# A perceiver layer on one core: keys transposed by DMA, value mixing packed on column tiles, new orders

## The chip, the cores and the metric

The kernel runs on one core of one Trainium2 chip. The time is the device time of one execution in microseconds (us), the median of several. A core has a matrix engine (TensorE, PE in the profile), a vector engine (VectorE, DVE), an activation engine (ScalarE, ACT), a general engine (GpSimd, POOL) and a queue engine (SyncE, SP), each with its own instruction stream, executed in order; they wait for one another by semaphores. SBUF is the on-chip memory, PSUM the memory that TensorE writes.

## The reference

x is 64 batches of 64 tokens of 128 numbers, the context 64 batches of 128 tokens of 96. Three blocks, each with a residual, follow one another:

```python
x = x + xattn(layernorm(x), ctx)   # 16 heads of 64, softmax over 128 context tokens, @ Wo + bo
x = x + attn(layernorm(x))         # 16 heads; scores from 5 sigmoid "path" bits a head: a tree similarity, causal softmax
x = x + ffn(layernorm(x))          # product-key experts: 8 heads; q@K1, q@K2 (32 keys each), the 10 best of the
                                   # 32x32 sums, softmax over them, gelu(x.w_down) weighted, times w_up
```

## The kernel before

The 4096 tokens are worked in 32 tiles of 128 tokens (two batches), t = 0 to 31. Every tile goes through some 100 named steps. `x.*` is the cross attention up to the probabilities (`x.q` queries, `x.w` their copies to SBUF, `x.s` scores, `x.x` maxima, `x.e` exponentials, `x.r` and `x.n` the division, `x.p` transposes of the probabilities, `x.t` their copies), `y.*` the mixing of the context and its output, `t.*` the tree attention, `k.*` the key scores and the choice of the best, `e.*` the experts: for each head h `e.s` adds the two key scores of all 1024 experts by a 0/1 matrix, `e.x` takes the exponential, `e.w` masks what is under the cut, `e.a` adds the heads up. The number in a name is a group of four heads (x, y) or a head (e).

The five order tables at the end of the file (`PE_ORDER` and so on, lines 1122 to 1148) set everything: `run` goes through iterations i, and in each one through the table's names in order; a name with lag L works on tile i - L. So one iteration, a period, holds steps of up to eight tiles, and each engine's instruction stream is fixed by its table. `BANK` (line 1151) gives each PE result its part of PSUM: x0, x1, t0, t1 (512 columns each), f0, f1 (1024 each). The waits at the head of a PE step, such as `after(pe, "y.u2", t - 1)`, wait until the previous user of that part has been read. Waits at the edges only (`at_ends`) don't matter inside.

The steps that the change touches:

- `keys_turn` (line 507), PE: eight transposes of 128x128 fp16 blocks of `us`, the key scores split into a high and a low fp16 part (`k.split`, line 949), into PSUM bank t1; `keys_sb` (line 642), ACT: one copy of the 128x1024 result to `usT`. The eight `e.s` of the tile use `usT` as weights (line 571).
- `mix` (line 384), PE: the transposed probabilities of a group times the context, one product of 96 rows of output and 512 columns (8 heads by 64 queries); `mix_sb` (line 630), ACT: the copy into `uT`, 96 partitions.
- `cross_out` (line 394), PE: a bias product and 16 products, one for each head, of 96 contracted rows. An fp32 product appears in the profile as two records.
- `queries`, `scores`, `probs_turn`, `sums`, `w_turn` and others: only which earlier step they wait for, with the new banks.
- SP's loads (lines 225 to 243): constants, then 16 small pieces of `awo`, then the steady loads `ld.x`, `ld.ct`, `ld.c`, `ld.xr` and the store `st.y`. ACT's queue loads six more weights (lines 652 to 657).
- the setup of the key weights and the fp16 split of the experts' `wdT` on DVE (`setup_keys`, line 828), done ahead of `y.res` of tile 0.

Of the kernel before, what the change touches and what calls it, by code (L numbers as in the profile page):

```python
# [8 lines left out]
M, CD = 128, 96  # L9
# [7 lines left out]
XHP, AHP = XH // 2, AH // 2  # L17
EC = NE // 128
# [10 lines left out]
def build(nc, a):  # L29
# [3 lines left out]
    with ctx:  # L33
# [3 lines left out]
        def sem(name):  # L37
# [24 lines left out]
        vo = sb("vo", [CD, XH, D])  # L62
# [20 lines left out]
        uT = sb("uT", [CD, XH, 2, N])  # L83
# [42 lines left out]
        own = {n: sem(n) for n in """wqk_load wvo_load key_load bias_load tree_load expert_load ones_set pool_set  # L126
            setup_ps setup_sb qk_split key_sb parts_done split_done
# [13 lines left out]
        def run(steps, order, begun=(), once={}):  # L141


            assert set(order) == set(steps), set(order) ^ set(steps)
            for i in range(NT + depth):
                for name, lag in order.items():
                    t = i - lag
                    if t == 0 and name in once:
                        once[name]()
                    if 0 <= t < NT and not (t == 0 and name in begun):  # L150
                        steps[name](t)
# [33 lines left out]
        def _(sp):  # L185
# [31 lines left out]

            def store(t):
# [11 lines left out]
            load_xr(0)  # L230
            sp.dma_start(bias[:, 512:640], a["bo"]).then_inc(own["bias_load"], 16)
            sp.dma_start(bias[:, 640:720], a["bp"]).then_inc(own["bias_load"], 16)
            for dst, name in ((wp, "wp"), (awv, "awv"), (rootc, "rootc"), (cneg, "cneg"), (ident16, "ident16")):
                sp.dma_start(dst[:], a[name]).then_inc(own["tree_load"], 16)
            sp.dma_start(wdT[:], a["wdT"]).then_inc(own["expert_load"], 16)
            sp.dma_start(sel[:], a["sel"]).then_inc(own["expert_load"], 16)
            sp.dma_start(wup[:], by_chunk(a["wup"])).then_inc(own["expert_load"], 16)
            for r in range(2):
                for c in range(AHP):
                    h = 2 * c + r  # L240
                    sp.dma_start(awo[N * r + AD * c:N * r + AD * c + AD, :], a["awo"][AD * h:AD * h + AD, :])\
                        .then_inc(own["tree_load"], 16)
            run(steps, SP_ORDER, begun=("ld.x", "ld.ct", "ld.c", "ld.xr"))
# [3 lines left out]
        def _(pe):  # L247
# [9 lines left out]
            def setup_vo():  # L257
                pe.wait_ge(own["wvo_load"], 16 * 2)
                pe.wait_ge(own["qk_split"], 4)
                for j in range(4):  # L260
                    if j >= 2:
                        pe.wait_ge(own["setup_sb"], j + 3)
                    head_pairs(j, wvT, wo, D, CD).then_inc(own["setup_ps"], 1)
# [93 lines left out]
            def probs_turn(k):  # L357
                def step(t):
                    if k == 0:
                        pe.wait_ge(s["x.e3"], t + 1)  # L360
                    elif k == 1:
                        pe.wait_ge(s["y.u0"], t + 1)
                    elif k == 2:
                        pe.wait_ge(s["x.e1"], t + 1)
                    elif k == 3:
                        after(pe, "t.csb", t - 1)
                        at_ends(pe, "x.w3", t)
# [6 lines left out]
            def mix(k):  # L374
                def step(t):
# [6 lines left out]
                    elif k == 3:  # L382
# [3 lines left out]
                    done(f"y.m{k}", pe.matmul(bank[BANK[f"y.m{k}"]][0:CD, :], c0[:, t % 2, k // 2, :], pT[:, k, :],  # L386
                                              start=True, stop=True))
# [6 lines left out]
            def cross_out(t):  # L394
                pe.wait_ge(s["y.u3"], t + 1)
                if t == 0:
                    pe.wait_ge(own["setup_sb"], 8)
                    pe.wait_ge(own["split_done"], 1)
# [10 lines left out]
            def t_turn(t):  # L409
                after(pe, "k.ksb", t - 1)  # L410
                at_ends(pe, "y.res", t)
                pe.wait_ge(s["t.norm"], t + 1)
                done("t.turn", pe.transpose(bank[BANK["t.turn"]][:, 0:128], xn2[:, t % 2, :], ident[:]))
            steps["t.turn"] = t_turn

            def paths_values(t):
# [16 lines left out]
            def feat_turn(t):  # L433
                pe.wait_ge(s["t.path"], t + 1)
                after(pe, "x.w3", t + 1)
                at_ends(pe, "t.sb", t)
# [45 lines left out]
            def tree_out(t):  # L482
                pe.wait_ge(s["t.div"], t + 1)
# [10 lines left out]
            def key_scores(t):  # L494
                pe.wait_ge(s["k.high"], t + 1)
                pe.wait_ge(s["k.low"], t + 1)
                if t == 0:
                    pe.wait_ge(own["key_sb"], 2)
                    pe.wait_ge(own["split_done"], 2)
# [7 lines left out]
            def keys_turn(t):  # L507
                after(pe, "y.res", t + 1)
                at_ends(pe, "t.csb", t)
                if t == 0:  # L510
                    pe.wait_ge(own["tree_load"], 16 * 21)
                pe.wait_ge(s["k.split"], t + 1)
                out = bank[BANK["k.kturn"]].bitcast(f16)
# [690 lines left out]
```

## Time and profile before

| | |
|---|---|
| runs | 1131.19, 1133.36, 1134.92 us; median 1133.36 |
| profiled execution | 1133.51 us, of it the span from the first to the last instruction 1131.7 us |
| granted TensorE clock, mean | 0.973 of full speed |
| busy | PE 89%, DVE 78%, ACT 85%, POOL 73% of the span |
| start, 31 periods, end | 69, 1009, 53 us |

A period is the time from a step of one tile to the same step of the next. Busy time is the union of an engine's instructions; idle time of an engine is shown with the instruction that ended it. The ends of matrix products are modelled, so consecutive groups on PE overlap in their shown times; the distance from start to start is what a group occupies.

### The profile page before, as it was taken

To read this page: it belongs to the slowest core of one execution; us is meant where nothing else is said; L and a number is where in the kernel's file an instruction comes from. 1 tells how busy PE (TensorE), PEld (TensorE's weight loads), DVE (VectorE), ACT (ScalarE), POOL (GpSimd) and SP (SyncE) were. 2 spreads that over 40 slices of the span, in tenths; PEclk is the share of its full clock that TensorE was granted. 3 is DMA by queue.
4 is the path that set the end of the run, shared out by engine and by line. 5 is a ranking of instruction groups with operands and counts; after the bars stand their busy time and mean duration, and the time that the engine had idled before them with its cause. 6 is when DMAs were issued, how large, how long until landed. Compare 5 with 4: busy or idle time off the path is not lost.

```text
span 1131.7 us, 34471 instructions
## 1 busy us (share of the span) xinstructions
PE 1009.9 (89%) x11656; PEld 771.8 (68%) x11656; DVE 883.9 (78%) x2941; ACT 960.1 (85%) x2251; POOL 824.9 (73%) x871
## 2 busy tenths in 40 slices
PE   3789899999999999999999999999999999999755
PEld 3666677777766777776677777766776777667433
DVE  2447788888888888888888888888888888888763
ACT  2579899999999999999999999999998999998642
POOL 0137777777987777788777777887777779777755
PEclk9999999999999999999999999999999999999865
DMA  6000000000000000000000000000000000000000
GB/s 158 13 13 12 14 15 4 16 16 16 17 13 16 11 9 16 16 16 14 16 16 7 13 16 17 16 14 16 17 4 16 16 16 15 13 14 7 4 3 6
DMA packets 36684, 18.79 MB, mean 17 GB/s; under 512 B 13632, under 2 KB 36256, under 8 KB 36512
## 3 DMA queue, kind: packets, MB, share of 16 engines
q1 hardware_dynamic: 32832, 14.91, 4.8%
q10 hardware_dynamic: 3680, 1.67, 0.6%
q8 instruction: 97, 1.59, 0.6%
q14 instruction: 75, 0.61, 0.2%
HBM read 14.47 MB, written 2.10 MB: 15 GB/s over the span
## 4 chain that ended last, share of the span: by engine, by line
DVE 29%; PE 27%; POOL 17%; issue 14%; ACT 10%; SPq 1%; DVEq 1%; POOLq 0%; DMA 0%; ACTq 0%
POOL wsum L1111 10%; PE psXT L386 9%; ACT p L698 6%; DVE mw L1003 6%; POOL feat L1095 5%; DVE cand L974 5%; DVE top L942 4%; DVE best L969 3%; DVE best L979 3%; PE psXT L351 3%; PE psXT L441 3%; PE psF L571 2%; PE psXT L370 2%; ACT am L737 2%; DVE us L954 1%
## 5 line engine op out<-in xcount | busy, mean ns | idle before, releaser
L1111 POOL TENSOR_TENSOR wsum<-wsum,mw 128x1024 f32<-128x1024 f32 x192 | 451.7, 2353 | 165.0 <-DVE mw L1003 159.4
L1003 DVE SCALAR_TENSOR_TENSOR mw<-psF,cut,ew 128x1024 f32<-128x1024 f32 x256 | 325.8, 1281 | 56.8 <-ACT ew L788 53.0
L788 ACT ACTIVATE ew<-psF,lnz 128x1024 f32<-128x1024 f32 x256 | 288.3, 1127 | 13.3 <-PE psF L571 10.2
L698 ACT ACTIVATE p<-psXT,negmax 128x128 f32<-128x128 f32 x512 | 182.2, 387 | 2.5 <-DVE negmax L876 2.5
L571 PE MATMUL psF<-sel,usT 128*128 128x512 f16 x512 | 157.0, 389 | 23.4 <-DVE mw L1003 20.4
L351 PE MATMUL psXT<-cT,q 96*128 96x128 f32 x1024 | 140.4, 281 | 22.8 <-ACT p L698 18.2
L351 PEld LDWEIGHTS psXT<-cT,q 96*128 96x128 f32 x1024 | 128.4, 194 | 42.9 <-ACT p L698 33.8
L1062 POOL TENSOR_TENSOR p<-p,rrow 128x512 f32<-128x512 f32 x128 | 131.2, 1035 | 19.0 <-DVE rrow L885 19.0
L386 PE MATMUL psXT<-pT,c 128*96 128x512 f32 x256 | 134.2, 611 | 0.8 <-ACT pT L604 0.8
L404 PE MATMUL psXT<-vo,uT 96*128 96x128 f32 x1024 | 121.2, 277 | 0.0
L698 ACT ACTIVATION_READ_ACCUMULATOR p<-psXT,negmax 128x1 f32 x512 | 117.2, 229 | 0.0
L404 PEld LDWEIGHTS psXT<-vo,uT 96*128 96x128 f32 x1024 | 116.9, 192 | 0.0
L286 PE MATMUL psXT<-xnT,qk 128*96 128x128 f16 x512 | 93.3, 223 | 8.3 <-DVE xnT L867 8.2
L1049 POOL TENSOR_TENSOR rstd<-mv,halfneg 128x1 f32<-128x1 f32 x96 | 52.7, 549 | 60.7 <-DVE mv L853 60.2
L876 DVE TENSOR_REDUCE negmax<-psXT 128x4 f32<-128x512 f32 x128 | 85.7, 669 | 12.0 <-PE psXT L351 11.8
L287 PE MATMUL psXT<-xnT,qk 128*96 128x128 f16 x512 | 93.1, 222 | 0.0
L288 PE MATMUL psXT<-xnT,qk 128*96 128x128 f16 x512 | 93.0, 222 | 0.0
L942 DVE MAX8 top<-psXT 128x8 f32<-128x32 f32 x512 | 53.3, 181 | 42.9 <-PE psXT L288 42.9
L370 PEld LDWEIGHTS psXT<-ident,p 128*128 128x128 f32 x512 | 62.9, 142 | 31.8 <-ACT uT L604 14.9
L604 ACT ACTIVATE uT<-psXT 96x512 f32<-96x512 f32 x128 | 75.3, 590 | 5.5 <-PE psXT L386 2.3
L1111 POOL TENSOR_TENSOR wsum<-mw 128x1024 f32<-128x1024 f32 x32 | 75.6, 2362 | 3.9 <-DVE mw L1003 3.9
L370 PE MATMUL psXT<-ident,p 128*128 128x128 f32 x512 | 77.5, 274 | 0.5 <-ACT p L698 0.5
(132 smaller groups left out, 2265.1 us busy)
## 6 DMA issues: line engine op xcount, KB each, us to landing
cT<-cT_dram SPq DMA_DIRECT2D x32, 96.0 KB, 2.0
c<-c_dram SPq DMA_DIRECT2D x32, 96.0 KB, 2.0
x<-x_dram SPq DMA_DIRECT2D x32, 64.0 KB, 2.2
xr<-x_dram SPq DMA_DIRECT2D x32, 64.0 KB, 1.8
y_dram<-y SPq DMA_DIRECT2D x32, 64.0 KB, 2.4
wqT<-wqT_dram SPq DMA_DIRECT2D x1, 512.0 KB, 5.9
wo<-wo_dram ACTq DMA_DIRECT2D x1, 512.0 KB, 9.8
wdT<-wdT_dram SPq DMA_DIRECT2D x1, 512.0 KB, 6.6
```

What stands on the lines that cost most here:

```text
L286: pe.matmul(out, left[:, 0, :], right[:, 0, :], start=not open_group, stop=False)
L351: mm = pe.matmul(bank[BANK[f"x.s{k}"]][:, i * M:i * M + M], q[:, b, h:h + 2, :].rearrange("c h q -> c (h q)"), cT[:, t % 2, b, :], start=T ...
L370: mm = pe.transpose(bank[BANK[f"x.p{k}"]][:, i * 128:i * 128 + 128], p[:, k, i, :], ident[:])
L386: done(f"y.m{k}", pe.matmul(bank[BANK[f"y.m{k}"]][0:CD, :], c0[:, t % 2, k // 2, :], pT[:, k, :], start=True, stop=True))
L404: mm = pe.matmul(out, uT[:, h, :, :].rearrange("c b q -> c (b q)"), vo[:, h, :], start=False, stop=(h == XH - 1))
L571: mm = pe.matmul(bank[BANK[f"e.s{h}"]][:, j * 512:j * 512 + 512], usT[:, t % 4, h, :], sel[:, j * 512:j * 512 + 512], start=True, stop=True)
L698: ins = act.activation(p[:, k, i, :], bank[BANK[f"x.s{k}"]][:, i * M:i * M + M], ACT.Exp, bias=negmax[:, k, i:i + 1], accum_out=rowsum[:, ...
L788: done(f"e.x{h}", act.activation(ew[:, h % NEW, :], bank[BANK[f"e.s{h}"]], ACT.Exp, bias=lnz[:, t % 4, h:h + 1]))
L942: ltop.link(dve.max(top[:, t % 2, k, :], keyed[:, k, :]))
L1003: done(f"e.w{h}", dve.scalar_tensor_tensor(out=mw[:, h % NMW, :], in0=bank[BANK[f"e.s{h}"]], scalar=cut[:, t % 4, h:h + 1], in1=ew[:, h % ...
L1062: done(f"x.n{k}", pool.tensor_tensor(p[:, k, :, :], p[:, k, :, :], rrow[:, k, :].unsqueeze(2).to_broadcast([128, 4, M]), ALU.mult))
L1111: done(f"e.a{h}", pool.tensor_tensor(wsum[:, t % 2, :], mw[:, 0, :] if h == 1 else wsum[:, t % 2, :], mw[:, h % NMW, :], ALU.add))
```

## The change

The keys' transpose becomes a step of SP, one transposing DMA a tile, from `us` to `usT`; PE's and ACT's steps for it are gone. The packed mixing: the contraction of 96 rows a head in `cross_out` is laid out over all 128 partitions. Of each four heads, three keep partitions 0 to 95 of their own slot, and the fourth's 96 rows are cut in three pieces of 32, one on partitions 96 to 127 of each slot; so `uT` and `vo` have 12 slots of 128 partitions. `mix` writes this layout by six products on column tiles. `y.u` copies 128 partitions by 384 columns. The orders, lags and banks of all engines are new, and with them the waits. In the start, loads are issued in the order of their use, `x` of tile 1 sixth, `awo` in two pieces, `wvT`, `wo`, `fwqT`, `fbqT` and `keys` from SP's queue; the DVE setup moves to `t.div` and `k.top` of tile 0.

```diff
-        vo = sb("vo", [CD, XH, D])
+        vo = sb("vo", [128, XH3, D])                 # XH3 = 12
-        uT = sb("uT", [CD, XH, 2, N])
+        uT = sb("uT", [128, XH3, 2, N])
+            def keys_turn(t):                        # on SP
+                sp.wait_ge(s["k.split"], t + 1)
+                for h in range(FH):
+                    after(sp, f"e.s{h}", t - 4)
+                after(sp, "k.kturn", t - 1)
+                sp.nop(nofuse=True)
+                sp.dma_start(usT[:, t % 4], us[:].rearrange("p h a b -> p (h a b)"), transpose=True)\
+                    .then_inc(s["k.kturn"], 16)
             load_x(0)
             sp.dma_start(wqT[:], by_chunk(a["wqT"])).then_inc(own["wqk_load"], 16)
             sp.dma_start(ident[:], a["ident"]).then_inc(own["wqk_load"], 16)
             load_ct(0)
             load_c(0)
-            load_xr(0)
+            load_x(1)
+            sp.dma_start(wvT[:], by_chunk(a["wvT"])).then_inc(own["wvo_load"], 16)
+            sp.dma_start(wo[:], by_chunk(a["wo"])).then_inc(own["wvo_load"], 16)
...
             def mix(k):                              # y.m
...
-                    done(f"y.m{k}", pe.matmul(bank[BANK[f"y.m{k}"]][0:CD, :], c0[:, t % 2, k // 2, :], pT[:, k, :],
-                                              start=True, stop=True))
+                    probs = pT[:, k, :].rearrange("m (g j q) -> m g j q", g=2, j=4)
+                    to = bank[BANK[f"y.m{k}"]][:, 0:6 * N].rearrange("c (g j q) -> c g j q", g=2, j=3)
+                    for j in range(3):
+                        cols = c0[:, t % 2, k // 2, 32 * j:32 * j + 32]
+                        pe.matmul(to[32 * j:32 * j + 32], cols, probs[:, :, 0:3, :], start=True, stop=True,
+                                  tile_position=(0, 32 * j))
+                        mm = pe.matmul(to[96:128, :, j, :], cols, probs[:, :, 3, :], start=True, stop=True,
+                                       tile_position=(0, 96))
+                    done(f"y.m{k}", mm)
...
             def cross_out(t):
-                for h in range(XH):
-                    mm = pe.matmul(out, uT[:, h, :, :].rearrange("c b q -> c (b q)"), vo[:, h, :],
-                                   start=False, stop=(h == XH - 1))
+                for i in range(XH3):
+                    mm = pe.matmul(out, uT[:, i, :, :].rearrange("c b q -> c (b q)"), vo[:, i, :],
+                                   start=False, stop=(i == XH3 - 1))
...
-            def keys_turn(t):                        # on PE
-                after(pe, "y.res", t + 1)
-                for h in range(FH):
-                    mm = pe.transpose(out[:, h * 128:h * 128 + 128], us[:, h, :, :].rearrange("p a b -> p (a b)"),
-                                      ident16[:])
...
             def mix_sb(k):                           # y.u
-                    to_sb(eng, f"y.u{k}", uT[:, 8 * (k % 2):8 * (k % 2) + 8, k // 2, :],
-                          bank[BANK[f"y.m{k}"]][0:CD, :].rearrange("c (h q) -> c h q", h=8))
+                    to_sb(eng, f"y.u{k}", uT[:, 6 * (k % 2):6 * (k % 2) + 6, k // 2, :],
+                          bank[BANK[f"y.m{k}"]][:, 0:6 * N].rearrange("c (i q) -> c i q", i=6))
...
-            def keys_sb(t):                          # on ACT
-                to_sb(eng, "k.ksb", usT[:, t % 4].rearrange("p h t -> p (h t)"), bank[BANK["k.kturn"]].bitcast(f16))
...
 PE_ORDER = {
+    "e.s2": 5, "e.s1": 5, "x.q3": 3, "x.s1": 3, "e.s0": 5, "t.fturn": 4, "e.s3": 5, "x.s3": 3, "t.sim": 4,
+    "e.s4": 5, "e.wturn": 6, "t.mix": 4, "x.p0": 3, "e.s5": 5, "t.cturn": 4, "x.p2": 3, "t.out": 4, "x.p1": 3,
+    "e.s6": 5, "y.m0": 3, "y.m2": 3, "y.m1": 3, "k.turn": 4, "e.s7": 5, "x.p3": 3, "k.key": 4, "y.m3": 3,
+    "x.turn": 2, "e.hid": 4, "y.out": 3, "x.q0": 2, "x.q1": 2, "e.out": 6, "x.q2": 2, "t.turn": 3, "x.s2": 2,
+    "t.pv": 3, "x.s0": 2,
 ACT_ORDER = {
+    "t.pexp": 4, "x.e2": 3, "k.lnz": 5, "e.x2": 5, "e.x1": 5, "x.e0": 3, "e.x0": 5, "t.fsb": 4, "e.x3": 5,
+    "x.e1": 3, "t.exp": 4, "e.x4": 5, "x.e3": 3, "x.t0": 3, "t.csb": 4, "e.x5": 5, "x.t2": 3, "x.t1": 3, "e.x6":
+    5, "k.norm": 4, "y.u2": 3, "k.high": 4, "y.u0": 3, "y.u1": 3, "x.t3": 3, "x.norm": 2, "e.x7": 5, "y.u3": 3,
+    "x.high": 2, "e.gelu": 4, "k.shift": 4, "x.w0": 2, "x.w1": 2, "t.norm": 3, "x.w2": 2, "t.sb": 3, "k.eb": 4,
+    "t.v": 3,
 DVE_ORDER = {
+    "e.add": 7, "k.z": 5, "t.path": 4, "x.x0": 3, "x.w3": 3, "e.w2": 5, "x.r2": 3, "e.w1": 5, "x.x1": 3, "x.r0":
+    3, "e.w0": 5, "e.w3": 5, "x.x3": 3, "x.r1": 3, "e.gate": 6, "t.div": 4, "e.w4": 5, "x.r3": 3, "t.res": 4,
+    "e.w5": 5, "x.stats": 1, "k.low": 4, "e.w6": 5, "k.top": 4, "k.split": 4, "x.low": 2, "e.w7": 5, "y.res": 3,
+    "k.cand": 4, "x.x2": 2,
 POOL_ORDER = {
+    "e.a7": 6, "t.feat": 4, "x.n2": 3, "x.n0": 3, "e.a1": 5, "x.n1": 3, "e.a2": 5, "x.n3": 3, "k.root": 4,
+    "e.a3": 5, "e.a4": 5, "e.a5": 5, "k.inner": 4, "e.a6": 5, "t.root": 3, "x.root": 1,
 SP_ORDER = {
-    "ld.x": 0, "st.y": 7, "ld.ct": 2, "ld.c": 2, "ld.xr": 2,
+    "st.y": 7, "ld.ct": 2, "ld.c": 2, "k.kturn": 4, "ld.x": 0, "ld.xr": 2,
```

The orders of before stand in the tables of the kernel (PE, for comparison: e.s1, x.s3, e.s0, t.fturn, x.s1, e.s3, t.sim, e.wturn, e.s4, x.p0, t.mix, e.s5, x.p2, t.cturn, y.m0, t.out, x.p3, y.m2, x.p1, e.s7, y.m3, k.turn, y.m1, x.turn, k.key, e.hid, y.out, e.s6, x.q1, x.q0, k.kturn, x.q2, e.out, x.s2, t.turn, t.pv, e.s2, x.s0, x.q3).

## Rows read from the trace of the kernel before

**Rows 1.** The instructions of line 485 (`t.out`): durations, first and last start

```profile
L485 PE MATMUL psXT<-awo,actxT x64: 275/287/422, 69.2 to 1078.5; 128*128 128x128 f32 x64
```

**Rows 2.** Windows view: one period; busy PE, PEld, DVE, ACT, POOL; granted clock; DMA share

```profile
600.24:632.79 32.55, 30.44 (x364) 23.42 (x363) 27.21 (x92) 29.71 (x71) 25.75 (x28) 1.00 0.06 15
```

**Rows 3.** Timeline of PE: start us, us shown, line, result<-operands, count

```profile
602.91 0.61 PE L515 MATMUL psXT<-ident,us 128*128 128x128 f16 x8
...
603.36 0.22 PE L286 MATMUL psXT<-xnT,qk 128*96 128x128 f16 x1
...
624.77 0.60 PE L370 MATMUL psXT<-ident,p 128*128 128x128 f32 x4
...
625.21 0.59 PE L571 MATMUL psF<-sel,usT 128*128 128x512 f16 x2
...
626.78 1.04 PE L386 MATMUL psXT<-pT,c 128*96 128x512 f32 x2
...
627.66 0.27 PE L300 MATMUL psXT<-ident,xn 128*128 128x128 f32 x1
...
630.07 3.79 PE L404 MATMUL psXT<-vo,uT 96*128 96x128 f32 x32
...
633.69 0.60 PE L571 MATMUL psF<-sel,usT 128*128 128x512 f16 x2
```

**Rows 4.** Chain of waits in that period: start us, us, what

```profile
602.56 1.19 DVE best L969 x8
...
607.16 1.29 DVE mw L1003
...
628.97 1.67 DVE top L942 x16
```

**Rows 5.** Timeline of ACT in the same period

```profile
603.56 1.02 ACT L604 ACTIVATE usT<-psXT 128x1024 f16<-128x1024 f16 x1 [0.53 <-PE psXT L515]
...
610.15 0.36 ACT L698 ACTIVATE p<-psXT,negmax 128x128 f32<-128x128 f32 x1
...
611.52 1.14 ACT L788 ACTIVATE ew<-psF,lnz 128x1024 f32<-128x1024 f32 x1
...
623.56 0.58 ACT L604 ACTIVATE uT<-psXT 96x512 f32<-96x512 f32 x1
...
630.27 1.28 ACT L778 ACT_TABLE_LOAD   x1 [0.65 <-PE psF L288]
...
633.90 0.60 ACT L759 ACTIVATE cand<-psXT 128x512 f32<-128x512 f32 x1
```

**Rows 6.** Timeline of PE around the tree's tiled steps

```profile
616.68 1.16 PE L454 MATMUL psXT<-featT 32*64 32x64 f32 x64
...
617.77 1.09 PE L583 MATMUL psF<-ident,wsum 128*128 128x128 f32 x8
...
619.13 0.60 PE L370 MATMUL psXT<-ident,p 128*128 128x128 f32 x4
...
619.69 1.11 PE L470 MATMUL psXT<-v,am 64*64 64x9 f32 x64
...
620.74 0.61 PE L571 MATMUL psF<-sel,usT 128*128 128x512 f16 x2
```

**Rows 7.** DMA issues: queue, size, median us from issue to landing

```profile
xr<-x_dram SPq DMA_DIRECT2D x32, 64.0 KB, 1.8
...
sel<-sel_dram SPq DMA_DIRECT2D x1, 256.0 KB, 6.9
```

**Rows 8.** Timelines of DVE and PE in the start

```profile
20.45 0.29 DVE L848 BATCH_NORM_STATS2 st<-x 128x6 f32<-128x128 f32 x1 [6.32 <-DMA x<-x_dram]
...
21.57 0.31 PE L286 MATMUL psXT<-xnT,qk 128*96 128x128 f16 x1 [8.24 <-DVE xnT L867]
...
44.52 3.79 PE L404 MATMUL psXT<-vo,uT 96*128 96x128 f32 x32
...
51.12 0.28 DVE L897 TENSOR_TENSOR x<-xr,psXT 128x128 f32<-128x128 f32 x1
```

More of the change, by code:

```diff
@@ L149, in run @@
                         once[name]()
-                    if 0 <= t < NT and not (t == 0 and name in begun):
+                    if 0 <= t < NT and (name, t) not in begun:
                         steps[name](t)
@@ L237, in _ @@
             sp.dma_start(wup[:], by_chunk(a["wup"])).then_inc(own["expert_load"], 16)
[L238 to L243, printed above, removed]
+            run(steps, SP_ORDER, begun=(("ld.x", 0), ("ld.x", 1), ("ld.ct", 0), ("ld.c", 0), ("ld.xr", 0)))
             sp.wait_ge(s["st.y"], 16 * NT)
@@ L482, in tree_out @@
             def tree_out(t):
-                pe.wait_ge(s["t.div"], t + 1)
+                pe.wait_ge(s["t.csb"], t + 1)
                 pe.wait_ge(s["t.csb"], t + 1)
@@ L551, in step @@
                     elif h == 2:
[L552 to L553 removed]
+                        pe.wait_ge(s["e.gelu"], t + 1)
                     elif h == 3:
@@ L578, in w_turn @@
             def w_turn(t):
-                after(pe, "e.w0", t + 1)
-                at_ends(pe, "e.w6", t)
+                after(pe, "e.w3", t + 1)
+                at_ends(pe, "e.add", t - 1)
                 pe.wait_ge(s[f"e.a{FH - 1}"], t + 1)
@@ L640, in copies @@
                         steps[name] = step
-            def keys_sb(t):
-                eng.wait_ge(s["k.kturn"], t + 1)
-                for h in range(FH):
-                    after(eng, f"e.s{h}", t - 4)
-                to_sb(eng, "k.ksb", usT[:, t % 4].rearrange("p h t -> p (h t)"), bank[BANK["k.kturn"]].bitcast(f16))
-            if "k.ksb" in order:
-                steps["k.ksb"] = keys_sb
         @block.scalar
@@ L1128 @@
+    "t.pv": 3, "x.s0": 2,
 }
 ACT_ORDER = {
-    "e.x1": 5, "x.e0": 3, "e.x0": 5, "t.fsb": 4, "e.x3": 5, "x.e3": 3, "t.exp": 4, "x.e1": 3, "x.t0": 3, "e.x4":
-    5, "t.csb": 4, "x.t2": 3, "y.u0": 3, "e.x5": 5, "x.t3": 3, "x.t1": 3, "k.norm": 4, "y.u2": 3, "k.high": 4,
-    "y.u3": 3, "y.u1": 3, "e.x7": 5, "x.high": 2, "e.gelu": 4, "k.shift": 4, "x.norm": 1, "x.w1": 2, "k.ksb": 4,
-    "x.w0": 2, "e.x6": 5, "t.norm": 3, "x.w2": 2, "t.sb": 3, "k.eb": 4, "t.v": 3, "k.lnz": 4, "t.pexp": 3,
-    "e.x2": 4, "x.e2": 2,
[3 rows of a table added]
@@ L1135 @@
+    "x.high": 2, "e.gelu": 4, "k.shift": 4, "x.w0": 2, "x.w1": 2, "t.norm": 3, "x.w2": 2, "t.sb": 3, "k.eb": 4,
+    "t.v": 3,
 }
 DVE_ORDER = {
-    "x.x0": 3, "x.w3": 3, "e.w2": 5, "e.w1": 5, "x.x3": 3, "x.r0": 3, "e.w0": 5, "x.x1": 3, "e.w3": 5, "x.r3":
-    3, "x.r2": 3, "e.gate": 6, "x.stats": 1, "x.r1": 3, "t.div": 4, "e.w4": 5, "t.res": 4, "e.w5": 5, "k.low":
-    4, "k.top": 4, "x.low": 2, "k.split": 4, "e.w7": 5, "y.res": 3, "k.cand": 4, "e.w6": 5, "k.z": 4, "e.add":
-    6, "x.x2": 2, "t.path": 3,
+    "e.add": 7, "k.z": 5, "t.path": 4, "x.x0": 3, "x.w3": 3, "e.w2": 5, "x.r2": 3, "e.w1": 5, "x.x1": 3, "x.r0":
@@ L1164 @@
 DVE_BIAS = "x.x2"
-DVE_KEYS = "y.res"
+DVE_KEYS = "t.div"
+DVE_DOWN = "k.top"
 def kernel(**inputs):
```

192 lines of the change are left out of this document (94 added, 98 removed), and 10 rows, old and new, of the table BANK.

## The prediction

> **What bounds the kernel now.** I read the repeated step first. Output matmul `t.out` starts first at 69.2 us, and its last record, the second of its product, at 1078.5 us [rows 1]: 31 periods of 32.55 us, 1009 of the 1131.7 us of the span. So the question is what one period becomes; before it lie 69 us, behind it 53 us. The windows view of one period shows no engine that is always busy: PE 30.4, ACT 29.7, DVE 27.2, POOL 25.8 of 32.55 us, TensorE's granted clock 1.00, that is 2.4 GHz, DMA 6% [rows 2]. PE's busy time is flattered by a tail: four transposes `x.p` show 0.60 us, but what follows starts 0.44 us after them [rows 3]; so 0.16 us of each group is pipeline. I use start to start throughout. So counted PE occupies about 29.4 us, ACT 29.7, and DVE, with the gaps inside its chains, some 27.7 to 28.5. The period is 3 us longer than any engine's work: it is a cycle that runs over several engines, each with a fixed order. The chain of waits shows it: `k.cand` (4.60 us from start to the next mask), the mask `e.w6`, later `k.top` [rows 4], with POOL's features and PE's mixes between. A change helps if it shortens that cycle or allows a shorter one.
>
> **The change in the period, part by part.**
> (1) PE's eight key transposes go: 8 in 0.45 us [rows 3]. ACT's copy goes: 1.02 us, some 0.92 start to start, and the 0.53 us that ACT idled ahead of it [rows 5].
> (2) `cross_out` has 12 head products in place of 16. 32 records take 3.62 us [rows 3], 0.113 each (two records a product), so 8 fewer save 0.90.
> (3) ACT's `y.u` reads 384 columns in place of 512. 1024 columns take 1.02 us and 512 take 0.58 [rows 5], 0.86 ns a column, so 0.11 us each, 0.44 in four.
> (4) The mix, most uncertain. Now one product of 512 columns, 0.88 us [rows 3]. Then six products on four column tiles, three of 384 and three of 128 columns: 1536 columns if one follows another, 384 on the fullest tile. At 0.88/512 us a column that is 2.64 us or 0.66. What tiles do side by side shows in the tree steps: 64 records of 64 columns on four tiles take 1.09 us, 17 ns each; 64 records of only 9 columns take 1.05, 16 ns each [rows 6]. A full-array record of 128 columns takes 113 ns, so one of 64 would take 57. Two row groups alone could bring that to 28, not to 17: column tiles do overlap, and both steps look bound by issue. Twelve records at 17 ns are 0.2 us of issue, no bound here. Proved is only 1.6 times what one stream does in one row group, so the bounds are 0.66 and 2.64/1.6 = 1.65 us. I take 0.66, nearest to what those rows do, and 0.1 us for each change into and out of tiles (x.p starts at 619.13, takes 0.44, and `t.mix` starts at 619.69 [rows 6]). `y.m0, y.m2, y.m1` stand together and `y.m3` apart, so four such gaps: 4 x 0.66 + 0.4 = 3.04 us against 3.52, a gain of 0.5; the bounds are 0.5 gained and 3.5 lost.
> The Trainium skill (TensorEngine Tiling (Array Packing), Key Properties) says that a change of tiling mode drains TensorE; the gap in rows 6 agrees. It also lists fast weight load as off under column tiling; if that made every weight load visible, the mixes would lose rather than gain, which is the first rival.
> (5) The transpose by DMA, 256 KB on SP's queue. No row shows a transposing DMA. Plain ones: 64 KB land in 1.8 us, 256 KB in 6.9 beside the other start loads [rows 7]. I take 5 us, bounds 1.8 and, if eight 128x128 blocks went one after another at 1.8 each, 14.4. Cover: `k.split` ends near 23.5 us in the walk below, `e.s2` is wanted at 31.3 and its consumer not before 33, so 7.8 to 9 us cost nothing. Meanwhile DVE does `e.w7`, `y.res` and `k.cand`. On SP the waiting issue stands ahead of `ld.x` and `ld.xr`, whose data are wanted most of a period later, and of the next store; none waits on the path.
> The Trainium skill speaks against this part: VectorE: DVE Perf Modes, The three transpose paths, gives 1309 ns for one 128x128 by DMA and 390 ns by TensorE; eight times the first is 10.5 us, an estimate beyond the cover, by which the period would grow by 1.5 to 2.7 us. Advanced Engine Details and Errata, X-Bar Transpose (TRN2), says that these DMAs are as fast as regular ones, which would leave it hidden. No row decides between them.
> (6) The orders. I walk the new cycle with start-to-start times. From the end of `x.x2` on DVE, ACT runs without a gap: four `x.e` at 1.37, five `e.x` at 1.00 (1.14 shown, 0.14 of it overlapped) [rows 5], `t.fsb` and `t.exp` 1.0 and 0.9 as steps of 1024 columns too, `x.t0` 0.48 (0.58 less 0.1 overlapped), two short `t.csb` 0.57, `k.lnz` 0.15: 13.6 us. PE then runs `t.out` 0.3, `x.p1` and `x.p3` 0.44 each, `e.s6` and `e.s7` 0.43 each, three mixes 2.64 at today's price, `k.key` (four products of 512 fp16 columns, 0.21 each) 0.86, `y.m3` 0.88, two small transposes 0.27, `e.hid` 24 x 0.056 = 1.35 [rows 3]: 8.0. ACT: two table loads, gelu and the step to `k.shift`'s start 3.63 [rows 5], `k.shift` 0.5. DVE: `k.cand` 4.60 [rows 4], `x.x2` 0.6. With four hand-overs of 0.1 to 0.2: 13.6 + 8.0 + 4.1 + 5.2 + 0.6 = 31.5 us. The old copy is in none of these legs; the path features, which now start the period on DVE and POOL, no longer wait behind `e.a6`. In the same walk `y.out` (2.8 us) ends just as `e.w7` does, POOL (25.8 us of work) is ready wherever it is asked, and `x.s1` costs a wait of about 1 us for the copy `x.w3` that sits directly ahead of it, which ACT's leg covers. With the mixes of (4) the cycle is 31.0; a hand walk misses waits, so I add 0.2: **31.2 us**, 1.35 less than now, 42 us over 31 periods.
>
> **The start.** The second x tile is asked for behind 32 other issues; DVE stands 6.32 us for it until 20.45, and the first query products start at 21.57 [rows 8]. With it sixth, `x.low` follows ACT's copy at 13.7, and the queries at about 14.2: 7.3 us. `wvT` and `wo` move to SP, land by some 14, and are wanted after the queries, four us later. The key and expert setup on DVE holds `y.res` of tile 0 until 51.12 though the cross output (44.52 + 3.79) is there at about 48.3 [rows 8]: 2.8 us; moved to `t.div` and `k.top` it meets a DVE that waits for PE, at a cost I put at 1. Sum 9, bounds 4 and 12. The tail keeps its POOL chain of seven sums; 0, bounds -3 and +3.
>
> **Sum.** The profiled execution took 1133.5 us (span 1131.7 and 1.8 around it), as the median of the runs, 1133.4. 1133.5 - 42 - 9 = 1082.5, say **1083 us**. Its own range is a period of 30.6 to 31.8, 1063 to 1103.
>
> **Rivals.**
> First, *column tiles overlap only in part*, the slower side. For it: all six products of a mix read the full 128 rows, the second record of a product waits for the first on its tile (0.33 us for 384 columns), and what queues behind it may not start; then a mix is 3 x (0.33 + 0.11) = 1.32 us. Against it: such a blocking would give the tree's 64-column records 28 ns, not 17 [rows 6]. All four mixes are in PE's leg, so the period is 31.7 (31.5 and the 0.2) + 4 x 0.44 + 0.4 = 33.9, the time 1133.5 + 31 x 1.3 - 9 = 1165 us; at 1.65 us a mix the period is 35.2 and the time 1206. It decides against the change from a period of 32.84, where the start's 9 us are used up: a mix of about 1.07 us beside the gaps.
> Second, *the DMA is late*. At 14.4 us it exceeds the 9 us by 5.4, the period is 36.6, the time 1250; slower from a landing of 10.6 us on. For it: nothing in the trace but the want of a row; against it: DMA engines at 6% [rows 2] and 64 KB in 1.8 us [rows 7]. By the skill's 10.5 us and a cover of 9 the same arithmetic gives 32.7 and 1129 us.
> Third, *the new order has waits of its own* that the walk doesn't see, `x.s1`, the three mixes waiting for `x.t2` and `x.t1`, whose copies follow `e.x5`. The period would be 32.2, the time 1133.5 - 11 - 9 = 1113. For it: three engines then have 28.0 to 28.5 us of work each, and evenly loaded engines leave less room to catch up; today's slack over the fullest engine, 2.9 us, would alone give 31.3.
> That the transposing DMA doesn't replace the PE and ACT steps isn't a case: both are gone from the program.
>
> **How the numbers follow.** Forecast 0.59, better still (period under 30.6) 0.06, third rival 0.18, first 0.11, second 0.06. A measurement of this kernel can tell 0.3%, 3.4 us. Of the third rival 0.03 falls within 3.4 us of before and 0.01 beyond: faster 0.79, same 0.03, slower 0.18. Range 1056 to 1128: it leaves out 0.02 below and 0.17 to 0.18 above, the two slower rivals.
>
> **What would show it.** The period, from the first and last `t.out`: near 31.2. Start to start of the mixes: 0.66 right, above 1.07 the first rival. The landing of the `usT` DMA: under 8 us, and no wait of `e.s2` for it; above 10, the second. ACT with no idle from `x.e2` to `t.csb`; DVE idle ahead of `k.cand` for `k.shift`. The first queries near 14 us. I am wrong if PE idles more than 3 us in a period for causes other than these.

## The result, and the profile after

| | before | after |
|---|---|---|
| median of four runs, us | 1133.2 (1131.2 to 1134.9) | 1119.9 (1118.7 to 1122.6) |
| ratio, 95% interval | | 0.989 (0.986 to 0.991) |
| profiled execution, us (span) | 1133.5 (1131.7) | 1122.6 (1119.4) |
| span's start to the first `t.out`, us | 69.2 | 60.6 |
| period, first to last `t.out`, over 31 | 32.56 | 32.53 |
| last `t.out` to the end, us | 53.2 | 50.3 |

The change gained 13 us, where 50 were forecast. In the profiled executions the start gave 8.6, the tail 2.9, the 31 periods together 1. First the records of `t.out` (line 519), to be held against [rows 1]:

```profile
L519 PE MATMUL psXT<-awo,actxT x64: 275/347/554, 60.6 to 1069.1; 128*128 128x128 f32 x64
```

In the windows view, with the columns of [rows 2], stand two neighbouring periods, and a stretch inside the second:

```profile
567.64:599.74 32.10, 29.06 (x386) 23.62 (x386) 27.39 (x92) 27.94 (x70) 25.89 (x27) 1.00 0.09 22
599.74:632.63 32.89, 30.35 (x386) 24.83 (x386) 27.41 (x93) 28.19 (x70) 25.91 (x27) 0.95 0.10 22
604.60:608.00 3.40, 3.40 (x17) 2.73 (x15) 2.60 (x4) 3.10 (x7) 2.16 (x3) 0.51 0.00 0
```

The work did leave: ACT has 27.9 us where [rows 2] show 29.7, PE 29.1 for 30.4. Yet the faster period is only 0.45 us shorter than before, and the slower one has a hole in TensorE's clock: 3.4 us at 0.51, that is 1.2 GHz. Between 100 and 1030 us the kernel before has one such stretch, this one has twelve, on 12 of 29 periods. From one `t.out` to the next the periods that a hole touches last 32.92 us in the mean, the others 32.13 (tiles 2 to 29). What stands around the hole, in PE's timeline (start, us, line, what; in brackets the idle time before it and its releaser), first in the undisturbed period:

```profile
567.98 0.60 PE L589 MATMUL psF<-sel,usT 128*128 128x512 f16 x2 [0.42 <-DVE y L1030]
...
570.43 1.13 PE L377 MATMUL psXT<-cT,q 96*128 96x128 f32 x8 [1.18 <-DMA cT<-cT_dram]
...
571.93 0.61 PE L589 MATMUL psF<-sel,usT 128*128 128x512 f16 x2 [0.37 <-DVE mw L1012]
572.38 1.04 PE L475 MATMUL psXT<-ident,feat 128*64 128x128 f32 x8
573.25 0.59 PE L589 MATMUL psF<-sel,usT 128*128 128x512 f16 x2
...
602.53 1.13 PE L377 MATMUL psXT<-cT,q 96*128 96x128 f32 x8 [1.18 <-DMA cT<-cT_dram]
...
604.03 0.61 PE L589 MATMUL psF<-sel,usT 128*128 128x512 f16 x2 [0.37 <-DVE mw L1012]
604.47 1.85 PE L475 MATMUL psXT<-ident,feat 128*64 128x128 f32 x8
606.12 1.06 PE L589 MATMUL psF<-sel,usT 128*128 128x512 f16 x2
```

In both periods PE waits three times in some five microseconds: 0.42 us ahead of `e.s1`, 1.18 ahead of `x.s1`, 0.37 ahead of `e.s0`. In one of them the clock then falls, and `t.fturn` takes 1.65 us start to start in place of 0.87. The long wait is the one of the third rival, for the copy `x.w3` on DVE; it ends at 602.39, just before `x.s1` starts. The profile writes "DMA cT" against it, the last of several semaphores, but no load of this tile's keys is under way there:

```profile
601.72 0.67 DVE L626 TENSOR_SCALAR q<-psXT 96x512 f32<-96x512 f32 x1
```

ACT in the undisturbed period, for [rows 5]:

```profile
589.84 1.28 ACT L785 ACT_TABLE_LOAD   x1 [0.88 <-PE psF L314]
...
593.47 0.60 ACT L766 ACTIVATE cand<-psXT 128x512 f32<-128x512 f32 x1
...
599.26 0.27 ACT L773 ACTIVATE ebest<-best 128x80 f32<-128x80 f32 x1 [2.09 <-DVE cut L993]
```

and DVE's `k.cand` in it, for the first row of [rows 4], with POOL's `e.a7` beside it:

```profile
594.20 1.18 DVE L978 MAX8 best<-cand 128x8 f32<-128x72 f32 x8 [0.48 <-ACT cand L766]
...
598.50 0.52 DVE L991 TENSOR_TENSOR cut<-best 128x8 f32<-128x8 f32 x1
599.06 0.17 DVE L993 TENSOR_SCALAR cut<-cut 128x8 f32<-128x8 f32 x1
599.14 0.69 DVE L885 TENSOR_REDUCE negmax<-psXT 128x4 f32<-128x512 f32 x1
599.74 0.28 DVE L1030 TENSOR_TENSOR y<-x,psF 128x128 f32<-128x128 f32 x1
```

```profile
596.64 2.35 POOL L1120 TENSOR_TENSOR wsum<-wsum,mw 128x1024 f32<-128x1024 f32 x1
```

`k.cand` lasts 4.94 us until `x.x2`, not 4.60. One instruction did it: the sum over 8 elements on line 991 took 0.52 us and ended within 0.03 us of POOL's addition. Before, POOL stood idle there: its next addition starts at 608.59, after 5.02 us without work, and `k.cand` ends at 607.16. All 32 of each kernel, with min/median/max in ns:

```profile
L982 DVE TENSOR_TENSOR cut<-best x32: 171/171/173, 86.3 to 1096.1; 128x8 f32<-128x8 f32 x32
```

```profile
L991 DVE TENSOR_TENSOR cut<-best x32: 171/528/685, 79.0 to 1085.7; 128x8 f32<-128x8 f32 x32
```

The transposing DMA, in the view of [rows 7], and the start, for [rows 8]:

```profile
usT<-us SPq DMA_TRANSPOSE x32, 3.2
```

```profile
12.26 0.28 DVE L857 BATCH_NORM_STATS2 st<-x 128x6 f32<-128x128 f32 x1
...
40.94 0.29 DVE L906 TENSOR_TENSOR x<-xr,psXT 128x128 f32<-128x128 f32 x1 [2.57 <-PE psXT L439]
```

```profile
13.38 0.31 PE L312 MATMUL psXT<-xnT,qk 128*96 128x128 f16 x1 [1.82 <-DVE xnT L876]
```

256 KB land, transposed, in 3.2 us (median of 32), and no step of PE waits for them. DVE no longer stands for the x tile, the first queries start 8.2 us earlier, and `y.res` of tile 0 waits for PE in place of the reverse.

### The profile page after: what moved, and what is told of

Read it like the earlier page. It is cut to its first block and busy times, and to the rows that moved or that the text cites. A ratio compares the mean times of both kernels' runs of the same rounds, so it can differ in the third digit from the quotient of the medians.

```text
span 1119.4 us, 36025 instructions
## 1 busy us (share of the span) xinstructions
PE 984.9 (88%) x12440; PEld 793.3 (71%) x12440; DVE 889.4 (79%) x2941; ACT 907.5 (81%) x2223; POOL 829.9 (74%) x871
## 5 line engine op out<-in xcount | busy, mean ns | idle before, releaser
L795 ACT ACTIVATE ew<-psF,lnz 128x1024 f32<-128x1024 f32 x256 | 283.6, 1120 | 15.0 <-PE psF L589 11.5
L589 PE MATMUL psF<-sel,usT 128*128 128x512 f16 x512 | 167.0, 411 | 33.0 <-DVE mw L1012 18.7
L377 PE MATMUL psXT<-cT,q 96*128 96x128 f32 x1024 | 144.5, 286 | 38.1 <-DMA cT<-cT_dram 31.8
L377 PEld LDWEIGHTS psXT<-cT,q 96*128 96x128 f32 x1024 | 132.7, 199 | 52.3 <-DVE q L626 41.8
L705 ACT ACTIVATION_READ_ACCUMULATOR p<-psXT,negmax 128x1 f32 x512 | 111.7, 218 | 0.0
L418 PE MATMUL psXT<-pT,c 128*32 128x384 f32 x768 | 98.7, 500 | 1.6 <-ACT pT L622 1.6
L420 PE MATMUL psXT<-pT,c 128*32 128x128 f32 x768 | 97.3, 277 | 0.0
L439 PE MATMUL psXT<-vo,uT 128*128 128x128 f32 x768 | 92.6, 278 | 0.0
L589 PEld LDWEIGHTS psF<-sel,usT 128*128 128x128 f16 x512 | 41.8, 101 | 66.1 <-DVE mw L1012 29.7
L439 PEld LDWEIGHTS psXT<-vo,uT 128*128 128x128 f32 x768 | 88.3, 192 | 0.0
L420 PEld LDWEIGHTS psXT<-pT,c 128*32 128x32 f32 x768 | 79.7, 111 | 0.3
```

The source lines that it names most:

```text
L377: mm = pe.matmul(bank[BANK[f"x.s{k}"]][:, i * M:i * M + M], q[:, b, h:h + 2, :].rearrange("c h q -> c (h q)"), cT[:, t % 2, b, :], start=T ...
L418: pe.matmul(to[32 * j:32 * j + 32], cols, probs[:, :, 0:3, :], start=True, stop=True, tile_position=(0, 32 * j))
L420: mm = pe.matmul(to[96:128, :, j, :], cols, probs[:, :, 3, :], start=True, stop=True, tile_position=(0, 96))
L439: mm = pe.matmul(out, uT[:, i, :, :].rearrange("c b q -> c (b q)"), vo[:, i, :], start=False, stop=(i == XH3 - 1))
L589: mm = pe.matmul(bank[BANK[f"e.s{h}"]][:, j * 512:j * 512 + 512], usT[:, t % 4, h, :], sel[:, j * 512:j * 512 + 512], start=True, stop=True)
L705: ins = act.activation(p[:, k, i, :], bank[BANK[f"x.s{k}"]][:, i * M:i * M + M], ACT.Exp, bias=negmax[:, k, i:i + 1], accum_out=rowsum[:, ...
```

## The experiments

All were timed beside the kernel before, in four groups in which that kernel's median was 1133.2 to 1135.3 us; so kernels of different groups are best compared by their ratios to it. Periods are from first to last `t.out` of the profiled execution; "holes" counts the stretches at 1.2 GHz between 100 and 1030 us.

| kernel | median us | ratio (95%) | period | holes |
|---|---|---|---|---|
| after | 1119.9 | 0.989 (0.986 to 0.991) | 32.53 | 12 |
| e1_busy | 1109.9 | 0.981 (0.975 to 0.986) | 32.23 | 1 |
| e2_swap | 1124.7 | 0.991 (0.989 to 0.993) | 32.64 | 16 |
| e3_a7 | 1108.2 | 0.977 (0.975 to 0.979) | 32.09 | 9 |
| e8_busy_a7 | 1100.5 | 0.971 (0.966 to 0.976) | 31.85 | 1 |
| e4_start | 1129.9 | 0.996 (0.995 to 0.997) | 32.63 | 1 |
| e7_oldorder | 1131.3 | 0.997 (0.995 to 0.998) | 32.63 | 1 |
| e14_orders | 1139.2 | 1.004 (1.003 to 1.006) | 33.08 | 0 |
| e9_unpacked | 1125.9 | 0.992 (0.990 to 0.994) | 32.68 | 4 |
| e10_turn | 1111.5 | 0.979 (0.977 to 0.981) | 32.14 | 0 |
| e12_turn_a7 | 1102.0 | 0.973 (0.970 to 0.977) | 31.87 | 0 |
| e13_turn_a7_csb | 1107.8 | 0.977 (0.975 to 0.978) | 32.04 | 0 |
| e11_more | 1131.3 | 0.998 (0.996 to 1.000) | 32.90 | 1 |

**Does the clock cost the period?** e2_swap puts `e.s1` behind `x.q3`, so that PE waits in one piece; e1_busy does the same and runs the products of `e.s1` four times over, work that changes nothing but how long PE is busy.

```diff
-    "e.s2": 5, "e.s1": 5, "x.q3": 3, "x.s1": 3,
+    "e.s2": 5, "x.q3": 3, "e.s1": 5, "x.s1": 3,
-                    for j in range(2):                       # e1_busy alone
+                    for j in range(8 if h == 1 else 2):
+                        j %= 2
```

> The changed kernel, with e.s1 moved behind x.q3 in PE's order and its two products done four times over, 1.3 us of work that changes nothing, in the place where PE waits for x.w3. Clock theory (PE's wait there lets the granted clock fall to 0.5 for 3.41 us in about every second period, and such a period is 33.0 instead of 32.1 us): the clock in the steady part is 1.00, all periods are 32.1, the time is some 13 us less, 1107. Rival, the waits themselves set the period and the clock is a side effect: the idle time only changes its name and the time stays at 1120, or grows by up to 1.3 us a period where PE is on the path, to 1160.

> The changed kernel with only e.s1 behind x.q3, its products done once. It tells the order from the filling work of e1. Clock theory: PE then stands some 1.9 us in one piece ahead of x.s1, the clock falls at least as often as in the changed kernel, time 1118 to 1126. Rival, the swap itself gave e1 its gain (x.q3 no longer waits behind e.s1, so x.w3 and x.s1 come earlier): 1110 or less.

The wait ahead of `x.s1` in PE's timeline of e1_busy, then of e2_swap:

```profile
607.05 1.89 PE L590 MATMUL psF<-sel,usT 128*128 128x512 f16 x8
609.42 1.13 PE L377 MATMUL psXT<-cT,q 96*128 96x128 f32 x8 [0.48 <-DMA cT<-cT_dram]
```

```profile
605.32 1.13 PE L377 MATMUL psXT<-cT,q 96*128 96x128 f32 x8 [1.77 <-DMA cT<-cT_dram]
```

600 us of the middle, as windows of after, e1_busy and e2_swap:

```profile
300.00:900.00 600.00, 545.67 (x7084) 443.92 (x7082) 508.30 (x1693) 518.00 (x1276) 478.59 (x506) 0.98 0.11 23
```

```profile
300.00:900.00 600.00, 563.72 (x7270) 451.98 (x7269) 512.15 (x1714) 520.45 (x1279) 484.00 (x507) 1.00 0.10 23
```

```profile
300.00:900.00 600.00, 543.99 (x7066) 443.40 (x7065) 506.27 (x1690) 516.29 (x1273) 477.39 (x504) 0.97 0.11 23
```

e1_busy and e2_swap have one order and differ by useless work alone. With it the clock holds, and 12 us are gained over e2_swap by the ratios (15 by the medians), whose interval it doesn't touch. The swap by itself is no gain: with a wait of 1.77 us in one piece there are 16 holes. In e2_swap too the periods that a hole touches last 32.95 us in the mean and the others 32.13; in e1_busy, without a hole, they last 32.17. So the holes are caused by PE's waits, each costs 0.8 us, and together they cost 0.3 to 0.4 us of each period. Against the changed kernel itself e1_busy gains 10 us by the medians, and their intervals just touch, because of one execution: the profiled one of e1_busy took 1122.3 us, the other three 1108.7 to 1111.0. In that one PE's products between 18 and 29 us took nearly twice as long as in the changed kernel, though the clock is given as 1.00 there, and its first `t.out` came at 69.6 us, not 60.6; why isn't known. The three that weren't profiled are shorter by more than these 9 us, so 32.23 may be slightly long for them.

**Does POOL's addition hold DVE?** e3_a7 runs `e.a7` behind `t.feat`; e8_busy_a7 has both this and e1_busy's edits.

```diff
-    "e.a7": 6, "t.feat": 4,
+    "t.feat": 4, "e.a7": 6,
```

> The changed kernel with e.a7 behind t.feat in POOL's order. Theory: the last sum of k.cand on DVE (128x8, 0.53 us here, 0.17 before the change) is held until POOL's e.a7 beside it ends; then it takes 0.17 again, and as k.cand is on the cycle the period falls by 0.36 us, 11 us in all, to 1109. Rival: the 0.53 is something of DVE itself and stays; the time stays at 1120, or rises a little as x.n2 starts 2.4 us later.

> The changed kernel with both edits, e.s1 behind x.q3 with its products done four times, and e.a7 behind t.feat. If the fall of the clock (0.3 to 0.4 us a period) and the held sum of k.cand (0.36) are separate costs, they add: period 31.8, time 1096 to 1099. If they are one cost seen twice, or the cycle then runs over another path, the time stays at the better of the two, 1108.

The sum of line 991 in e3_a7:

```profile
L991 DVE TENSOR_TENSOR cut<-best x32: 171/172/174, 79.2 to 1072.1; 128x8 f32<-128x8 f32 x32
```

All 32 are at 0.17 us again, and the period is 0.44 shorter, with 9 holes still there. Taken without a hole it is 31.79 in place of 32.13, shorter by 0.34, just what the sum had lost; the rest of the 0.44 is fewer holes. Both edits together give 31.85, 0.68 less than the changed kernel, where 0.30 and 0.44 apart make 0.74: the effects add, nearly. 1100.5 us is the fastest median here.

**What is the start worth alone?** e4_start is the kernel before with the new order of loads, the second x tile loaded sixth, and the key and expert setup behind `t.div` and `k.top`.

```diff
-            load_xr(0)
+            load_x(1)
...
-DVE_KEYS = "y.res"
+DVE_KEYS = "t.div"
+DVE_DOWN = "k.top"
```

> The kernel before with only the new start: the loads in the new order and the setup on DVE moved to t.div and k.top; steady orders as they were. If the start alone gives what the changed kernel gained ahead of its first t.out (60.6 against 69.2 us), this gives 1133 - 9 = 1124, and the steady period stays 32.55. Rival, the steady part of the changed kernel gained too and the start less: 1129 or more.

4.6 us by the ratio (3.4 to 5.9), where 9 were expected: the first `t.out` comes at 63.7, 5.5 us earlier than before, and the 31 periods together are 2 us longer. In the changed kernel it comes 3.1 us earlier still; e14_orders, below, which adds the new orders to the new start and has all the old work, has it at 61.1, so most of that belongs to the orders.

**What are the lighter steps worth, and in which order?** e7_oldorder has the transposing DMA, the packed mixes and the new start in the old orders. e14_orders has the new orders and start with all the old work (transposes on PE, copy on ACT, mixes of one product). e9_unpacked is the changed kernel with the old mixes, e10_turn the changed kernel with the old transposes and copy, put where they fit:

```diff
-    "y.out": 3, "x.q0": 2, "x.q1": 2, "e.out": 6, "x.q2": 2,                 # PE, e10_turn
+    "y.out": 3, "k.kturn": 4, "x.q0": 2, "e.out": 6, "x.q1": 2, "x.q2": 2,
-    "k.shift": 4, "x.w0": 2,                                                 # ACT
+    "k.shift": 4, "k.ksb": 4, "x.w0": 2,
-    "ld.c": 2, "k.kturn": 4, "ld.x": 0,                                      # SP
+    "ld.c": 2, "ld.x": 0,
```

> All parts of the change (start, packed mixing, transposing DMA) in the old orders and banks, with the DMA on SP ahead of ld.xr. Theory, what was removed lies off the old cycle, and the mixes standing apart there gain nothing (4 x 0.66 and eight changes into and out of tiles at 0.1 is 3.4 us against 3.5): period 32.4 to 32.6, only the start's 9 us are gained, 1121 to 1125. Rival, work removed from the fullest engines pays wherever it stands (PE 1.4, ACT 1.9 us a period): period 31.2, 1083. Second rival, the DMA delays the step e.s2 that uses it in the same iteration: period above 33, above 1140.

> New orders, banks and start alone: the mixing unpacked as before and the keys transposed by TensorE and ACT, so all the work of the kernel before, without the transposing DMA. Theory, in the new orders too the removed work was largely off the cycle: period 32.4 to 32.8, time 1115 to 1128, faster than before by the start and little else, and the clock holds at 1.00. Rival, the new orders need both reliefs: period 33.5 or more, 1150 and above.

> The changed kernel (new orders, transposing DMA) with the mixing as it was: one product of 512 columns a group, 16 heads, y.u of 96x512. Theory, in the new order the mixes and y.out lie on the cycle: the mixes cost 0.3 us more, y.u 0.44 on ACT and y.out 0.9 ahead of y.res, so the period grows by 0.6 to 1.2 us, 1139 to 1157. Rival, packing is off the cycle here too, as in the old orders: 1120, within 4 us.

> The changed kernel with the keys transposed by TensorE and copied by ACT again (eight transposes behind y.out, the copy behind k.shift, x.q1 behind e.out for the bank), and no transposing DMA. Theory, ACT idles 2.1 us ahead of k.eb and PE 1.9 us in two pieces, so the 0.9 us copy and the 0.45 us of transposes fill idle time and the DMA gains next to nothing: 1116 to 1130; the clock may even hold better. Rival, the new orders are possible only by the DMA's relief: the period grows by the copy's 0.9 us or more, 1148 and above. Second rival, the DMA itself costs something (256-byte packets beside other traffic): below 1112.

Periods, by what is in the new orders:

| | old mixes | packed mixes |
|---|---|---|
| transposed by PE and ACT, placed as in e10_turn | 33.08 | 32.14 |
| transposed by DMA | 32.68 | 32.53 (32.10 where the clock holds) |

In the old orders all the lighter work together gives nothing (32.63, as e4_start has with the new start alone): it was off that cycle. In the new orders with the old work the kernel is slower than before; 1115 to 1128 us had been expected, from removed work being off the cycle there too, and that is refuted. The packed mixes then bring 0.94, the DMA 0.40 without them and nothing beside them. Packing was expected to be worth 0.6 to 1.2 beside the DMA; it is worth 0.15, and 0.4 where the clock holds. The DMA costs the holes: e10_turn, which does more work, is 8 us faster than the changed kernel, their intervals apart (0.977 to 0.981, 0.986 to 0.991). Below 1112 us had been said to speak for a cost of the DMA itself, by its traffic; but e10_turn's period is that of the changed kernel's periods without a hole (32.12 and 32.13 in the mean), which leaves nothing for it. Its window of the same 600 us, and PE's waits ahead of `x.s1` and `e.s0` in it:

```profile
300.00:900.00 600.00, 547.66 (x7374) 450.06 (x7376) 512.36 (x1699) 539.10 (x1316) 482.39 (x506) 1.00 0.05 14
```

```profile
562.68 1.03 PE L591 MATMUL psF<-sel,usT 128*128 128x512 f16 x4
...
565.26 1.13 PE L366 MATMUL psXT<-cT,q 96*128 96x128 f32 x8 [0.88 <-DMA cT<-cT_dram]
...
566.76 0.61 PE L591 MATMUL psF<-sel,usT 128*128 128x512 f16 x2 [0.37 <-DVE mw L1022]
```

PE's waits there are 0.88 and 0.37 us, and the one ahead of `e.s1` is gone: 1.25 in sum, where the changed kernel has 1.97. That they are shorter because the transposes, which stand some 10 us ahead, use that time up is my reading; the edit also moved `e.out`, so it is less clean a test than e1_busy. How often a hole comes doesn't follow from the waits alone: e9_unpacked and e3_a7 both wait 1.18 and 0.37 or 0.38, and have 4 and 9 holes.

**Can the cycle be shortened further?** e12_turn_a7 is e10_turn with e3_a7's edit. e13_turn_a7_csb also copies the tree context ahead of the mix inputs, so that `t.out` starts sooner; e11_more is e8_busy_a7 with that and two more exchanges.

```diff
-    "x.t0": 3, "t.csb": 4,                    # e13_turn_a7_csb, e11_more
+    "t.csb": 4, "x.t0": 3,
-    "e.gelu": 4, "k.shift": 4,                # e11_more, ACT
+    "k.shift": 4, "e.gelu": 4,
-    "x.q2": 2, "t.turn": 3, "x.s2": 2,        # e11_more, PE
+    "x.q2": 2, "x.s2": 2, "t.turn": 3,
```

> The kernel e10 (new orders, packed mixing, keys transposed by TensorE and copied by ACT, no transposing DMA) with e.a7 behind t.feat, no work that does nothing. Theory: the held sum costs 0.36 us a period here too, 1111.5 - 11 = 1100, with the clock at 1.00 throughout. If the held sum is hidden in this order: 1111.

> e12 with t.csb ahead of x.t0 on ACT. In the changed kernel's trace PE waits 0.5 us for t.csb, and ACT could do it 0.25 us earlier: if PE's leg from t.out is on the cycle, 0.25 us a period below e12, 1090 to 1094. If x.t0, 0.3 us later, takes its place ahead of y.m0, or k.norm decides: as e12, within 4 us.

> Both edits of e8 and three more swaps in the orders: t.csb ahead of x.t0 and k.shift ahead of e.gelu on ACT, x.s2 ahead of t.turn on PE. By the legs of the changed kernel's trace t.csb comes 0.25 us earlier, and k.cand no longer waits for k.shift, which comes behind 3.6 us of gelu and table loads (DVE idles 0.48 us there). If both are on the cycle: 0.4 to 0.7 us a period below e8, 1076 to 1086. If x.w0 and x.w1, which come 0.5 us later behind the gelu, take the place of k.shift, at e8's time or above, 1096 or more.

e12_turn_a7 gives 1102.0 us with no useless work, 31.87 a period and no hole. The other two are misses: 1090 to 1094 and 1076 to 1086 us had been expected. The period of e13_turn_a7_csb is 0.17 longer than that of e12_turn_a7, though the intervals of the two times overlap. `x.t0` and what hangs on it come later; the waits of DVE for `xn3T` between 300 and 1000 us (total, times, longest), in e12_turn_a7 and then in e13_turn_a7_csb:

```profile
DVE xn3T L886 <- ACT xn3T L770: 17.0, 22, 1.4
```

```profile
DVE xn3T L886 <- ACT xn3T L770: 27.6, 22, 1.9
```

In e11_more ACT now stands 2.41 us for DVE's `k.split` before it may shift the key scores, with gelu and the query copies queued behind, and later waits where it did not:

```profile
634.54 0.60 ACT L767 ACTIVATE cand<-psXT 128x512 f32<-128x512 f32 x1 [2.41 <-DVE us L966]
...
642.45 0.28 ACT L729 ACTIVATE v<-psXT 128x128 f32<-128x128 f32 x1 [0.54 <-PE psXT L464]
```

So in both kernels a step moved ahead to shorten one leg made others wait longer. The three exchanges of e11_more weren't tested apart; the wait points at `k.shift`.

## Why the prediction was wrong

The time lies in the range and the direction is right, but the case that came is the third rival (a period of 32.2, 1113 us), at 32.53 and 1120, and not the forecast of 31.2 and 1083. That the kernel got faster at all is owed to the start and the tail: the periods, from which 42 of the 50 us were to come, gave 1. By its own steps:

- **The start**: right in sum, 8.6 us where 9 were forecast, but by some luck: the start's own edits give 5.5 of it (e4_start), the rest comes with the new orders. The first queries came at 13.4 us (forecast 14.2).
- **The tail**: 0 forecast, -2.9 measured, within its bounds. It goes with the new orders: from the last `t.out` to the end are 53.2 us in e7_oldorder and 51.3 in e14_orders.
- **The mixes**: right within 0.2 us. The three that stand together take 2.24 us from start to start of what follows (forecast 3 x 0.66 and the change out of tiles, 2.08), `y.m3` 0.79 (0.76). The first rival is out. PE's timeline, with the place of `k.key` and the bias product that follows `e.hid`:

```profile
582.93 0.51 PE L418 MATMUL psXT<-pT,c 128*32 128x384 f32 x1
...
585.17 0.30 PE L525 MATMUL psXT<-ident,xn 128*128 128x128 f32 x1
...
585.74 0.60 PE L396 MATMUL psXT<-ident,p 128*128 128x128 f32 x4
586.32 0.38 PE L537 MATMUL psXT<-bias,ones 96*128 96x512 f16 x1
...
587.28 0.51 PE L418 MATMUL psXT<-pT,c 128*32 128x384 f32 x1
...
588.07 0.33 PE L326 MATMUL psXT<-ident,xn 128*128 128x128 f32 x1
...
589.57 0.22 PE L437 MATMUL psXT<-bias,ones 96*128 96x128 f16 x1
```

- **The DMA**: 3.2 us, below the 5 that I took and far below the cover of 7.8 to 9; the second rival is out. The Trainium skill (VectorE: DVE Perf Modes, The three transpose paths) had led to an estimate of 10.5 us for the eight blocks; the trace disagrees. It agrees with the other page, which calls such DMAs as fast as regular ones (Advanced Engine Details and Errata, X-Bar Transpose (TRN2)): the plain 256 KB of `sel` land in 3.9 us in the same trace. But "hidden" was not the end of it: without packed mixes the DMA is worth 0.40 us a period, beside them nothing, and PE's waits then cost clock.
- **The cycle**: this step failed. The walk of part (6) gave 31.0, and the period that its cycle has while the clock holds is 32.10. Leg by leg, from the rows above (a hand-over of 0.15 counted in each leg that has one):

| leg, start to start | walk | measured |
|---|---|---|
| `x.x2` ends (567.65) to `t.out` (581.67), ACT | 13.9 | 14.0 |
| `t.out` to gelu's table load (589.84), PE | 7.65 | 8.17 |
| to `k.shift` (593.47), ACT | 3.63 | 3.63 |
| to `k.cand` (594.20) | 0.65 | 0.73 |
| to `x.x2` (599.14), DVE | 4.60 | 4.94 |
| its end (599.74) | 0.6 | 0.6 |
| sum | 31.0 | 32.1 |

The path through the engines was the right one; its legs are longer by 1.1 us, for which I had added 0.2. A third of that is the held sum, tested by e3_a7. The 0.5 on PE is small pieces, read from the trace and not tested: what follows the three mixes starts 0.16 us later than forecast, `k.key` starts 0.58 us after the `x.p` before it and not 0.44, and the table load starts 0.27 after the end of `e.hid`, where a hand-over was put at 0.15. The third rival named the right place, PE's wait of about 1 us for `x.w3` (1.18 measured), and I let it stand at no cost because "ACT's leg covers" it. In time it does: e1_busy still waits there, and its period is within 0.13 us of the undisturbed one. So that wait lengthens no leg of the cycle; it costs through the clock, which ACT's leg doesn't cover.
- **The clock**: no step of the forecast had it. From 32.10 to 32.53 over 31 periods are 13 us; e1_busy wins back 10. With it and the held sum in the sum, the forecast would have been a period of 31.2 + 0.43 + 0.34 = 32.0 and 1083 + 31 x 0.77 = 1107 us; the rest, 0.56 a period, is what else the walk had too short, and no run tests it.

One sum of the prediction is off: periods of 30.6 to 31.8 make 1064 to 1101 us, not 1063 to 1103. Nothing hangs on it.

That removing work gave nothing is thus three things: in the old orders it lay off the cycle; in the new ones it pays for orders that by themselves cost 0.45 us a period (33.08 beside 32.63, e14_orders beside e4_start); and of what is left, the clock and the held sum take 0.8.

## What to carry to other kernels

A step that is off the longest cycle gives nothing when it is made cheaper, and it may have been what kept TensorE at 2.4 GHz; before taking work off PE, look at its waits around the place that it leaves, and afterwards at the granted clock. When an order is changed, look at what runs beside each short instruction of the longest cycle, POOL's long additions above all, and move the one that isn't urgent. A hand walk of a cycle over three engines was 3% short here (1.1 us), nearly as much as the change was to gain (1.35): put that into the forecast, not only into the range.

## What the runs showed of the hardware

- A `tensor_tensor` of DVE with 8 columns and both inputs in SBUF took 0.52 us in place of 0.17 and ended with POOL's addition of 1024 columns that ran beside it. The `max8` and `match_replace` before it, under the same addition, kept their times: from the start of the second eight `max8` (597.29) to the sum are 1.21 us, as in the kernel before (605.66 to 606.87). The Trainium skill (SBUF — State Buffer, Who interferes with whom) says that a DVE instruction with two SBUF inputs contends with a GpSimd instruction that reads SBUF, and that the port pair they share is an exclusive lock; the trace agrees.
- Waits of PE of 0.42, 1.18 and 0.37 us in five, in a stretch where it is otherwise busy, were followed by 3.4 us at 1.2 GHz in 12 periods of 29; waits of 1.77 and 0.37 (e2_swap) by 16 such stretches. Half the clock costs 0.8 to 1.1 us each time, as `t.fturn`, `e.s3` and `x.s3` fall into it.
- A DMA that transposes 256 KB of two-byte values within SBUF landed in 3.2 us (3.1 to 5.4). Its issue holds SP for 1.25 us where plain ones take 0.33 to 0.51:

```profile
591.42 1.25 SPq L226 DMA_TRANSPOSE usT<-us  x1
592.79 0.51 SPq L194 DMA_DIRECT2D x<-x_dram  x1
593.79 0.33 SPq L200 DMA_DIRECT2D xr<-x_dram  x1
```

- Three column tiles of 32 columns and a fourth, all reading 128 rows, overlap: 1536 columns in six products (12 records) take 0.66 us and about 0.1 for a change of tiling.
